# A graph network's third edge stage: sums signalled by halves

## The reference

```
hn = leaky(layernorm(h) @ node_W.T + node_b)          # per node, 32 wide
he = leaky(layernorm(edge_z) @ edge_W.T + edge_b)     # per edge, 32 wide
msg = concatenate([hn[src], he])                       # per edge, 64 wide
emb_edge = leaky(layernorm(msg) @ red_W.T + red_b)    # per edge, 64 wide
msg_sum = segment_sum(emb_edge, dst) + emb_local
z = msg_sum / (deg + 1)
```

## Time and profile before

| | |
|---|---|
| median of 3 runs | 5187.8 us (5182.0 to 5188.24) |
| the profiled execution | 5181.95 us, its span 5180.1 us |
| busy over the span | PE 4219.9 us (81%), DVE 4154.5 us (80%), ACT 1913.8 us (37%), POOL 3375.1 us (65%) |
| the third edge stage | about 2330 to 3358 us of the span |

### The profile page before, as it was taken

How to read it: one execution, slowest core, us unless ns; L and a number is a source line. 1 busy time by engine, 2 the same in 40 slices (tenths; PEclk the granted TensorE clock), 3 DMA queues, 4 the chain that set the end, 5 groups by cost and what they waited for, 6 DMA issues and landing times. The chain is left out here.

```text
span 5180.1 us, 101586 instructions
## 1 busy us (share of the span) xinstructions
PE 4219.9 (81%) x28712; PEld 2871.7 (55%) x28712; DVE 4154.5 (80%) x7696; ACT 1913.8 (37%) x6351; POOL 3375.1 (65%) x2950
## 2 busy tenths in 40 slices
PE   5999999999788888857777677658888888199998
PEld 3555555555444444435555555535555455199998
DVE  6777778777688888857777877778888888899998
ACT  2555555555301111124444444311111111277774
POOL 5787778777277777736555555367777777055554
PEclk7999999999888988868888888889999999599998
DMA  4333333333122222212112222145455545011111
GB/s 113 87 86 84 82 83 87 85 86 84 28 50 51 51 51 55 44 27 52 49 46 50 48 47 50 24 117 135 135 134 134 146 134 139 31 47 48 49 48 33
DMA packets 493009, 379.51 MB, mean 73 GB/s; under 512 B 345991, under 2 KB 379152, under 8 KB 492888
## 3 DMA queue, kind: packets, MB, share of 16 engines
q1 hardware_dynamic: 395352, 288.65, 19.7%
q0 software_dynamic: 90560, 83.37, 9.4%
q10 hardware_dynamic: 6976, 6.23, 0.4%
HBM read 341.76 MB, written 36.12 MB: 73 GB/s over the span
## 5 line engine op out<-in xcount | busy, mean ns | idle before, releaser
L1069 POOL DMA_INDIRECT edge_src_rows<-table_wh,edge_gather_idx x806 | 1002.3, 1244 | 299.8 <-issue 282.5
L933 POOL DMA_INDIRECT edge3a_src_rows<-table_h,edge3a_gather_idx x808 | 762.5, 944 | 326.9 <-issue 245.1
L1098 PE MATMUL edge_sums_ps<-edge_onehot_src,edge_halves 128*128 128x512 bf16 x4840 | 871.0, 329 | 11.8 <-DVE edge_onehot_src L1174 11.8
L933 POOL DMA_INDIRECT table_cat<-table_hn,table_gather_idx x592 | 588.7, 994 | 419.7 <-PE edge_cat_t_ps L1779 218.6
L1460 POOL DMA_INDIRECT edge_src_rows<-table_h,edge_gather_idx x608 | 616.3, 1014 | 273.4 <-issue 178.3
L1098 PEld LDWEIGHTS edge_sums_ps<-edge_onehot_src,edge_halves 128*128 128x128 f16 x4840 | 396.0, 98 | 428.7 <-DVE edge_onehot_src L1174 8.5
L2099 PE MATMUL edge3a_z_ps<-Wz,edge3a_both_ends_t 128*128 128x396 f32 x1616 | 586.3, 514 | 9.5 <-DVE edge3a_terms L2192 7.4
L2511 PE MATMUL edge3b_sums_ps<-edge3b_onehot,edge3b_weighted 128*128 128x128 f32 x4848 | 571.2, 278 | 7.0 <-DVE layers_accT L2549 5.1
L2428 POOL TENSOR_TENSOR edge3b_weighted<-edge3b_src_rows,edge3b_alpha 128x1920 f32<-128x1920 f32 x101 | 350.2, 3467 | 344.3 <-DVE edge3b_alpha L2528 246.4
L2511 PEld LDWEIGHTS edge3b_sums_ps<-edge3b_onehot,edge3b_weighted 128*128 128x128 f32 x4848 | 552.0, 193 | 12.7 <-DVE layers_accT L2549 5.3
L2192 DVE SCALAR_TENSOR_TENSOR edge3a_terms<-edge3a_z_ps,att_z 128x792 f32<-128x792 f32 x404 | 391.3, 977 | 152.7 <-PE edge3a_z_ps L2099 152.1
(11 more groups left out here) (366 smaller groups left out, 7986.8 us busy)
## 6 DMA issues: line engine op xcount, KB each, us to landing
edge_dst_row<-in_dst_row SPq DMA_DIRECT2D x102, 512.0 KB
edge3a_dst_row<-in_dst_row SPq DMA_DIRECT2D x102, 512.0 KB
edge_window<-table_wh SPq DMA_DIRECT2D x816, 32.5 KB
edge3a_window<-table_h SPq DMA_DIRECT2D x816, 32.0 KB
edge_edge_attr<-in_ea SPq DMA_DIRECT2D x101, 256.0 KB
kept_rows<-edge3a_src_rows SPq DMA_DIRECT2D x101, 256.0 KB
edge3b_src_rows<-kept_rows SPq DMA_DIRECT2D x101, 256.0 KB
edge_edge_attr<-in_ea SPq DMA_DIRECT2D x101, 128.0 KB, 2.2
```

The costliest lines, as they stand in the source:

```text
L933: nc.gpsimd.indirect_dma_start(self.slot(b, j), None, self.table[:, :], bass.IndirectOffsetOnAxis(ap=self.idx[b][:, j:j + 1], axis=0)).the ...
L1069: nc.gpsimd.indirect_dma_start(g[q][:, j, :], None, k.t_wh[:, :], bass.IndirectOffsetOnAxis(ap=idx[q][:, j:j + 1], axis=0)).then_inc(gathe ...
L1098: mm = pe.matmul(acc[:, i, 0:w], halves[q][:, j, a, :, :].rearrange("p h d -> p (h d)"), hot[:, o:o + w], start=first and a == 0, stop=False)
```

## The change

TensorE increments `sums_ready` behind the fourth and behind the eighth matmul of `sum_up`, so twice a batch. VectorE's `add` waits for `2n - 1` ahead of its register loads and first four additions, and for `2n` ahead of the fifth. Nothing else is changed.

```diff
@@ sum_up
                     for j in range(B):
                         mm = pe.matmul(sums[:, j, :], msg[h][:, j, :], oh[h][:, j, :], start=True, stop=True)
-                    mm.then_inc(sums_ready, 1)
+                        if j in (B // 2 - 1, B - 1):
+                            mm.then_inc(sums_ready, 1)
@@ add
                 def add(n, h, t, m=0, hots=range(0)):
-                    dve.wait_ge(sums_ready, n)
+                    dve.wait_ge(sums_ready, 2 * n - 1)
                     for j, base in enumerate(window_starts(nc, k, DVE, t, h)):
+                        if j == B // 2:
+                            dve.wait_ge(sums_ready, 2 * n)
                         dve.wait_ge(added[j - 2], n if j != 1 else n + 1)
```

## The result

The changed kernel takes 5098.5 us (median of six, 5093.99 to 5100.7) where the kernel before takes 5186.1 (six, 5182.0 to 5191.46): a ratio of 0.9832, 95% interval 0.9823 to 0.9842, so 87 us less. 5100 was predicted. The profiled execution took 5098.32 us, its span is 5096.5 us, 83.6 less than that of before.

A forecast was written before the change was run, and what follows sets the result against it. No engine is full; engines waiting for each other set the stage. 25 x 4.2 = 105 us, less 25 x 0.8 = 20 for the clock, plus 3 at the end: 88 us off the 5187.8 median, 5100; range 5076 to 5142.

The forecast's parts named there:

- The loop: VectorE's additions hold back the message, the message TensorE's lines 1795 and 1735, and these the next additions.
- The size at each place: First addition 1.60 us earlier at `b` 1; additions end 3.3 in all earlier at `b` 2; 4.2 at `b` 3.
- The clock: TensorE's low-clock stretch moves onto a message and its 13 multiplications (line 1742), costing 2.4 us in one round of three.
- The sign of records far above 390 ns at the 13: In the profile after, line 1742's multiplications would show some records far above 390 ns, where all took 379 to 390.
- the second rival: Low clock moves onto the 13 multiplications in most rounds, losing 2.3 of each 4.2 us: 5138 us, chance 0.15.
- The new wait for the root: At `b` 3 VectorE's `edge_row` waits for ScalarE's root, taking back 0.5 us on VectorE but not on TensorE.
- The loads: Eight register loads behind VectorE's wait: 0.87 us from signal to first addition, not spared but moved forward with the wait.
- The fifth addition: Its own wait for the second signal costs nothing at `b` 1 and 0.1 us at most at `b` 2.
- The ends: The last two batches, where VectorE also waits, gain half of a slow group, 1.6 us, twice: 3 us.
- The rival that the clock holds: TensorE's clock stays up with shorter waits, so the full 4.2 us a round come: 108 us, 5080, chance 0.15.
- No change: The eighth sum still holds the first addition, or the second wait replaces the first: 5188 us, chance 0.03.
- slower: Low clock covers both groups of 13, message and sums of `b` 3 every round: 7.5 us against 4.2, 5270, chance 0.04.

The follow-up runs named there:

- e6: The changed kernel with VectorE's eight register loads moved ahead of its wait for the first half of the sums: 5094.9 us, ratio 0.9831.
- e8: The changed kernel with the early half wait at `b` 1 only, VectorE waiting for the second signal ahead of its loads elsewhere: 5165.72 us, ratio 0.9968.
- e7: The kernel before, one signal a batch, with the eight register loads moved ahead of VectorE's wait: 5140.08 us, ratio 0.9922.
- e5: The changed kernel with eight matmuls that nobody reads (fillers) in TensorE's long wait at `b` 0: 5080.89 us, ratio 0.9805.
- e9: The changed kernel with 8, 6 and 4 matmuls that nobody reads in TensorE's waits at `b` 0, 1 and 2: 5073.14 us, ratio 0.9775.

## Why the prediction was right

*The loop.* That the additions, the message and the sums make one loop, and that an earlier first addition passes right round it, held: what VectorE gained behind the three groups of sums is the round's whole gain to 0.1 us.

*The size at each place.* 1.60 us were predicted at `b` 1 and 1.25 came. The term mis-sized is the half of the group: I halved 3.21 us, but that group began at the low clock and ended at the full one, so its first half took 1.96 us (2.83 less 0.87), not 1.60. Groups of 3.45 and 3.63 us have the first addition after the same 2.83 us (2850.34 to 2853.17 in the next round), which shows that only the first half counts. At `b` 2 1.7 were predicted and 1.72 came, but with the group at the full clock, which had not been foreseen: there VectorE's own work ahead of the additions was the limit, and in the slow rounds it waits 0.5 to 0.9 us more. At `b` 3 it was 0.94 and 0.88. In all 4.2 against 3.85.

*The clock.* 0.8 us a round were taken off, and the reason given was wrong: the 13 multiplications were never slow, as their row shows. The low clock cost something else, a slow message and slow sums at `b` 2 in two of four rounds, 0.6 and 1.0 us: 0.4 on average. 4.2 - 0.8 and 3.85 - 0.4 are both 3.4, so the figure of 5100 is as near as it is by luck, by two errors that cancel. The sign of records far above 390 ns at the 13 did not come, and VectorE's waits for the sums were 44.8 us where some 35 were due (0.85 us at `b` 1, not 0.5). That the 13 can be hit is shown by e6 and e8, whose rounds of that kind are longer than their fast ones by 1.5 us and more; the second rival was a real danger and was missed only by where the groups came to lie.

*The new wait for the root* at `b` 3 came in one round of four alone, 0.7 us, where 0.5 was predicted for all.

*The loads.* The 0.87 us were taken from three places and read as mostly register loads; e7 measured 0.72 for them. *The fifth addition* waits for 0.1 us at most, as predicted. *GpSimd* stayed hidden with 127 us left. *The ends* gave about 4.7 us in place of 3: 85 us are found in the stage, 80.3 in its 24 rounds (24 x 3.35), 2.7 ahead of the first and 2.0 behind the last, against 83.6 of the span.

*The rival that the clock holds* fell: 37.12 is the best round, and the 36.76 us a round that it stands for (40.96 less 4.2) were reached only with fillers, on average 36.77 us in e5 and 36.63 in e9. *No change* and *slower* did not come. What a second increment costs is not shown: the sum of the round closes to 0.1 us, and 26 ns in each of four batches would be just that. TensorE itself is not held up by it, since the sums of `b` 3 start 1.75 us ahead of the 13 multiplications behind them in every round of both kernels. So the price of 2.6 us by the Trainium skill (TensorE: Matmul & The Clock Gate, section The cost: per-tile semaphore tail) is neither shown nor refuted here.

## What to carry to other kernels

When an engine waits for a group of results that come one by one, a signal at the half is worth the half that it no longer waits for, at the speed of that moment: read the first half's time, not half of the whole, and look at what stands behind the wait (register loads, here 0.72 us) before the first use. In this loop of engines that wait for each other, every shortening moved the stretches of low TensorE clock to other groups, so that gains did not add up: one wait shortened alone was worth 17 us where 30 were due, and in the changed kernel waits made shorter still by the loads ahead were worth nothing. Look for the groups that must not be hit, here the 13 multiplications, and count what they cost at the low clock before trusting a sum.

## What was not expected of the hardware

Rounds repeat with their clock in a fixed pattern, one round of 40.96 us before, four rounds of 37.13, 37.15, 37.76 and 38.14 after, two of 38.4 and 40.1 in e7. Fillers of 1.16 to 2.05 us in a wait of 2 to 4 us kept the message behind them at the full clock in most rounds (17 to 19 of 24 at `b` 1), but not always the sums behind it. And two chips took 6075 and 6160 us for the kernel before, 17 to 19% more than 5186, at the same duration of an addition and a gather, with stretches of up to 1.7 us in which four engines stand still together.
